# Attention layer on one core: the first two steps' probabilities are moved one step at a time, and three pair stores go to ScalarE's queue

## What is computed

```python
q = query @ w_q                       # 32 batches x 64 queries, 16 heads of 64
kv = context @ w_kv                   # 32 batches x 1601 keys, 192 channels in
scores = jnp.einsum('bhqd,bhkd->bhqk', q, k) * SCALE
attn = jax.nn.softmax(scores, axis=-1)
out = jnp.einsum('bhqk,bhkd->bhqd', attn, v)
```

## Time and profile before

| | |
|---|---|
| median of three runs | 2347.87 us (2347.65 to 2348.88) |
| the profiled execution | 2348.63 us, of which the span of instructions 2346.8 us |
| TensorE busy | 2290.6 us, 98% of the span |
| GpSimd, VectorE, ScalarE busy | 1647.7, 1815.5, 1541.4 us |
| DMA engines, SyncE's queue (q1) | 76.9% of 16 engines' span |
| start of the first scores / first product | 121.11 / 158.99 us |

### The profile page before, as it was taken

One profiled execution on the slowest core, in us unless ns is written; L12 is line 12 of the kernel. 1 busy time (PEld: TensorE's weight loads), 2 busy tenths in 40 slices (PEclk: granted clock), 3 DMA queues, 4 the chain that ended last, 5 costly groups with the idle time before them and its releaser, 6 DMA issues.

```text
span 2346.8 us, 43941 instructions
## 1 busy us (share of the span) xinstructions
PE 2290.6 (98%) x13696; PEld 2098.0 (89%) x13696; DVE 1815.5 (77%) x3664; ACT 1541.4 (66%) x2696; POOL 1647.7 (70%) x858
## 2 busy tenths in 40 slices
PE   7989999999999999999999999999999999899999
PEld 5769999999999999999999999999999998878788
DVE  7867777777777777777777777777777777789884
ACT  6756666666666666666666666666666666565444
POOL 4248888888888888888888888888888886421111
PEclk9999999999999999999999999999999999999999
DMA  8988888888888888888888888888888886987000
GB/s 228 261 222 197 195 191 199 199 199 199 199 198 199 200 199 200 199 200 199 200 199 201 199 200 199 199 200 200 200 200 199 200 197 157 212 202 197 1 10 28
DMA packets 410274, 438.97 MB, mean 187 GB/s; under 512 B 82529, under 2 KB 380897, under 8 KB 410209
## 3 DMA queue, kind: packets, MB, share of 16 engines
q1 hardware_dynamic: 391248, 425.66, 76.9%
q10 hardware_dynamic: 18960, 12.49, 2.3%
HBM read 167.42 MB, written 52.43 MB: 94 GB/s over the span
## 4 chain that ended last, share of the span: by engine, by line
PE 41%; POOL 31%; issue 17%; DVE 4%; SPq 3%; DMA 1%; ACT 1%; ACTq 0%; POOLq 0%; DVEq 0%
POOL p_pt_lo L667 17%; PE p_scores L1557 14%; PE p_acc L1577 9%; POOL p_nat L694 5%; PE p_acc L1579 4%; POOL p_q_lo L679 4%; POOL p_ct_lo L675 3%; POOL p_ct_hi L686 3%; SPq L462 2%; PE p_cols L1625 2%; PE p_scores L1683 2%; PE p_scores L1729 2%; PE p_cols L1716 2%; PE p_scores L1641 1%; PE p_scores L1507 1%
## 5 line engine op out<-in xcount | busy, mean ns | idle before, releaser
L667 POOL TENSOR_TENSOR p_pt_lo<-p_landed,p_pt_hi 128x768 fp32r<-128x768 f32 x504 | 991.0, 1987 | 326.3 <-ACT p_pt_hi L893 326.3
L1577 PE MATMUL p_acc<-p_nat,p_pt_hi 128*128 128x384 f32 x3024 | 890.4, 361 | 16.0 <-POOL p_pt_lo L667 14.8
L1579 PE MATMUL p_acc<-p_nat,p_pt_lo 128*128 128x192 f32 x3024 | 759.6, 251 | 0.0
L929 ACT ACTIVATE p_prob<-p_scores,p_negmax 128x800 f32<-128x800 f32 (+1 forms) x512 | 470.9, 925 | 382.5 <-DVE p_negmax L1266 382.5
L1557 PE MATMUL p_scores<-p_ct_hi,p_q_hi 128*128 128x512 f32 (+2 forms) x2048 | 703.0, 347 | 4.2 <-ACT p_prob L929 4.0
L1557 PE MATMUL p_scores<-p_ct_hi,p_q_lo 128*128 128x512 f32 (+2 forms) x2048 | 702.6, 346 | 0.0
L1577 PEld LDWEIGHTS p_acc<-p_nat,p_pt_hi 128*128 128x128 f32 x3024 | 569.3, 188 | 24.8 <-issue 14.1
L1579 PEld LDWEIGHTS p_acc<-p_nat,p_pt_lo 128*128 128x128 f32 x3024 | 578.8, 191 | 0.0
L893 ACT ACTIVATE p_pt_hi<-p_landed 128x768 fp32r<-128x768 f32 x504 | 398.6, 838 | 176.2 <-PE p_acc L1581 128.7
L1276 DVE STREAM_TRANSPOSE turned<-p_prob 128x1536 f32<-128x1536 f32 x256 | 452.6, 1768 | 0.0
L1557 PEld LDWEIGHTS p_scores<-p_ct_hi,p_q_hi 128*128 128x128 f32 x2048 | 388.4, 190 | 50.6 <-ACT p_prob L929 6.2
(11 more groups left out here) (253 smaller groups left out, 3128.6 us busy)
## 6 DMA issues: line engine op xcount, KB each, us to landing
p_landed<-turned SPq DMA_DIRECT2D x2032, 104.0 KB, 2.3
resid<-in_ctx SPq DMA_DIRECT2D x128, 288.0 KB, 5.0
o_scratch<-resid SPq DMA_DIRECT2D x256, 96.0 KB, 2.6
p_stage<-qk_scratch SPq DMA_DIRECT2D x31, 512.0 KB, 3.9
p_stage<-qk_scratch SPq DMA_DIRECT2D x62, 256.0 KB, 4.2
qk_scratch<-p_out_a SPq DMA_DIRECT2D x30, 512.0 KB, 5.3
p_stage<-in_ctxT SPq DMA_DIRECT2D x31, 401.0 KB, 4.7
p_stage<-in_ctxT SPq DMA_DIRECT2D x62, 200.5 KB, 5.6
```

What stands on the lines that cost most here:

```text
L667: nc.gpsimd.tensor_tensor(pt_lo[:, t0:t1, :, :], by_tile(slot, t0, t1), bits(pt_hi[:, t0:t1, :, :]), ALU.subtract).then_inc(pt_lo_done, 1)
L929: nc.scalar.activation(prob[:, lo:hi], scores[:, S0 + lo:S0 + hi], ACT.Exp, bias=negmax[:, par:par + 1], accum_out=rowsum[:, par, h:h + 1] ...
L1577: nc.tensor.matmul(acc[k % 2][:, 0:2 * DC], pt_hi[:, t, :, :].rearrange("p i x -> p (i x)"), x[:, t, :], start=t == 0, stop=False, skip_gr ...
L1579: nc.tensor.matmul(acc[k % 2][:, 0:DC], pt_lo[:, t, :, :].rearrange("p i x -> p (i x)"), x[:, t, 0:DC], start=False, stop=False, skip_grou ...
```

## The change

Three things. The first pair (steps 0 and 1) is moved by `move_first`, one step at a time: 16 DMAs for step 0 as soon as it is transposed, and 16 for step 1, with the two parts of `load_qk` around them. Staging slot 0 is laid one `landed` slot further back, so that `landed`'s first slot is free of it (slot 3, which is laid behind it, shifts as well). And pair 29 is stored by ScalarE too, in step 1. The waits follow: high(0) waits for `moved_first`, high(1) and all later for `moved` as before, and VectorE's step 4 waits for both.

```diff
+        assert put.at <= landed_at + 4 * PADDED
+        put.at = landed_at + 4 * PADDED
+        first_slot = slot(0)
         assert put.at >= landed_at + 2 * 4 * PADDED
         last_slot = slot(3)
...
+        def move_first(eng, j, done):
+
+            slot = slice(j, j + 1)
+            for i in range(G):
+                for g in range(G):
+                    dst = landed[g * R:(g + 1) * R, slot, i, :, :].rearrange("p s t x -> p s (t x)")
+                    eng.dma_start(dst, turned[i * R:(i + 1) * R, slot, g * GK:(g + 1) * GK]).then_inc(done, 16)
...
-                    if begins:
-                        sp.wait_ge(qk_stored[0], GP // SLOTS * 32)
-                    move(n * PPB, 0, begins)
+                    if not begins:
+                        move(n * PPB, 0, False)
...
-            for h in range(2):
-
-                sp.wait_ge(ct_a_done, 3 + h)
-                load_qk(1, h, stage[:, h, :])
-                store_queries(GP - LATE + 1 + h)
+
+            sp.wait_ge(ct_a_done, 3)
+            load_qk(1, 0, stage[:, 0, :])
+            store_queries(GP - LATE + 1)
+            sp.wait_ge(turned_done, 1)
+            move_first(sp, 0, moved_first)
+            sp.wait_ge(ct_a_done, 4)
+            load_qk(1, 1, stage[:, 1, :])
+            sp.wait_ge(turned_done, 2)
+            sp.wait_ge(qk_stored[0], GP // SLOTS * 32)
+            move_first(sp, 1, moved[0])
             passes(sp, body)
...
-                act.wait_ge(moved[slot // 2], count)
+                if fresh:
+                    act.wait_ge(moved_first, MOVES)
+                else:
+                    act.wait_ge(moved[slot // 2], count)
...
-                    if first and j in (LATE - 3, LATE - 2):
+                    if first and LATE - 4 <= j < LATE - 1:
                         g = GP - LATE + 1 + j
...
                 dve.wait_ge(exp_done, s + 1)
+                if first and j == 4:
+                    dve.wait_ge(moved_first, MOVES)
```

More of the change, by code:

```diff
@@ L227, in whole_layer @@
         slot = lambda i: (put(f"out_a{i}", [P, CB, 2, NQ]), put(f"out_b{i}", [DCB, CB, 2, NQ]))
-        first_slot = slot(0)
         x_ident = put("x_ident", [P, P])
         x_stats, x_mv, x_std = put("x_stats", [P, TT, 6]), put("x_mv", [P, TT, 2]), put("x_std", [P, 4, TT])
+        assert put.at <= landed_at + 4 * PADDED
+        put.at = landed_at + 4 * PADDED
+        first_slot = slot(0)
         assert put.at >= landed_at + 2 * 4 * PADDED
@@ L336, in whole_layer @@
         turned_done = sem("turned_done")
-        moved, moved_last = [sem("moved0"), sem("moved1")], [sem("moved_last0"), sem("moved_last1")]
+        moved_first, moved, moved_last = sem("moved_first"), [sem("moved0"), sem("moved1")], [sem("moved_last0"), sem("moved_last1")]
         pt_hi_done, pt_lo_done, last_lo_done = sem("pt_hi_done"), sem("pt_lo_done"), sem("last_lo_done")
```

## The result

Median of five runs: 2406.73 us (2405.74 to 2409.66) after, 2347.87 us (2347.17 to 2353.6) before, measured beside it. The ratio is 1.0252, with a 95% interval of 1.0241 to 1.0263: 58.9 us slower. I had forecast 2347.5 with a range to 2352.2.

The account below looks back on a forecast made before the run. TensorE's pace was taken as the bound, so only start-up idleness counted: 1.9 us gained at product(2) less 1.6 for the clock, 0.3 off the median 2347.87, giving 2347.5 us; own range 2344.8 to 2350, 8-in-10 range 2343.7 to 2352.2.

Parts of the forecast that it names:

- From there on all waits for TensorE's pace again: After product(2), later moves land ahead of need (182.0 against 184.2 us), so batches keep 58.46 us.
- the whole sum: At product(2): 1.9 us gained, 1.6 lost to the clock, leaving 0.3 us; no change forecast.
- Both signs that I had named for an error: Wrong if product(2) starts before 171 or after 177 us, or if later batches are not at 58.46 us.
- my rivals: Start-up alternatives: whole pause goes, 2340.5 us (with a milder way 0.12); full stalls, 2352.2 (0.17); every single stalls, 2358.4 (0.11).
- T: Time at which SyncE has issued the second single-step group of moves: forecast 153.3 us, 153.20 before.
- the rival in which the 5.7 us of stalls come back in full: SyncE's first moves: T 157.9, product(2) at 177.9, 4.3 us lost with the clock, 2352.2 us; chance 0.17.
- the rival after: Each single DMA stalls as the first move's did: T 164.1, product(2) at 184.1, 2358.4 us; chance 0.11.
- the issue of a single: SyncE's issue of single-step moves at the start: 10.6 us for each group of 16.
- the row of rows 7: Earlier trace's row for single-step DMAs, taken as the measure of the new groups: 16 issues in 10.58 us, median 592 ns.
- The 0.95 us for 64 KB: Skill figure cited against the change at the first moves: 15.2 us a group, T 162.5, some 9 us slower.
- 1.6 us lost in product(2): TensorE's clock falls in the 5.5 us pause before product(2), costing the same 1.6 us as before, now behind it.
- high(2) released by the landing: At the start, ScalarE's high(2) waits for the move of steps 2 and 3 to land, at about 170.4 us.

Follow-up runs that it names:

- split-only one: The kernel before with the first group's split and the slots' shift, third pair still stored by SyncE, loop start 334: 2353.38 us, ratio 1.002.
- 335: The whole changed kernel with 40 more do-nothing instructions ahead of SyncE's loop: 2350.21 us, ratio 1.0012 to the kernel before.
- 295: SyncE instructions ahead of its loop in the changed kernel, 2406.73 us, and in the kernel before with 13 more waits, 2402.91 us, ratio 1.023.
- 312: The kernel before with 30 more do-nothing instructions ahead of SyncE's loop: 2385.97 us, ratio 1.0155.
- 279: The kernel before with the slot shift and third pair stored by ScalarE, no split, no padding: 2347.30 us, ratio 0.9989.
- 282: SyncE instructions ahead of its loop in the kernel before, unedited: 2347.87 us.
- 287: The whole change without padding, half of the first step's 16 moves issued by ScalarE instead of SyncE: 2348.35 us, ratio 1.0004.
- 288: The kernel before with 6 more do-nothing instructions ahead of SyncE's loop: 2348.68 us, ratio 1.0001.
- 336: Three kernels with the second batch's six row loads issued by ScalarE: changed kernel 2347.85 us, kernel before 2346.42, store and slots without split 2345.09.
- 339: The kernel before with only the slots' shift and third pair stored by ScalarE, no split, padded: 2345.20 us, ratio 0.9982.
- 342: The kernel before with 60 more do-nothing instructions ahead of SyncE's loop: 2346.37 us, ratio 0.9989.

## Why the prediction was wrong

- **The step that failed** is "From there on all waits for TensorE's pace again", and with it the whole sum, which ended at product(2). I had treated the batches behind the start as untouched, since no instruction in them changed. Their place in SyncE's instruction memory changed, and each turn lost 4.15 us, 13 times. Both signs that I had named for an error came: batches not at their 58.46 us, which is this one, and product(2) after 177, which is the start's.
- **None of my rivals held it.** All of them worked on the start. I had counted the issues that the change adds in time, never in length of the code ahead of the loop, and I had not asked how much SyncE could lose in a turn. The trace of before had the answer to the second: 3.4 us in 117.
- **The start went by a rival, not by my forecast.** T was to be 153.3 and was 158.4; the rival in which the 5.7 us of stalls come back in full had 157.9. Product(2) was to be at 173.3 and came at 178.15, where that rival had 177.9. (T lies just past 158.3, from which on I had given it to the rival after, whose own T was 164.1.) The term that was mis-sized is the issue of a single: 13.86 and 11.82 us a group in place of 10.6 each, 4.5 us of the 5.1; the two issues of `load_qk` between them took 2.2 in place of 1.2. The group of the earlier trace rows had loads beside it on ScalarE's queue and no pair store; these had pair stores. That is 0.87 and 0.74 us an issue for 0.66 (where the prediction says that it takes the row of rows 7, rows 8 is meant).
  The 0.95 us for 64 KB that the Trainium skill lists (DMA: Bandwidth & Descriptors, section Bandwidth) is the time in which the DMA engines are busy with one transfer that GpSimd issued, so it was no measure of an issue. What an issue took here is 0.66 us in the group of the earlier trace rows, 0.74 and 0.87 in the changed kernel and 1.00 in the split-only one.
- **The clock was counted once and fell twice.** I had product(0) at full speed behind its shorter wait and 1.6 us lost in product(2). After a wait of only 2.24 us product(0) took 5.40 us too. It cost nothing at the end, since product(2) waited 5.2 us for the DMA anyway; in product(2) the loss was 1.8.
- **Right** were product(0) (153.0 for 153.2, its wait 2.24 for 2.2), high(2) released by the landing with a pause of 5.2 us behind it (5.5 forecast), and the clock at half in it (0.50 from 176 to 180 us).
- **With the loop's place taken out** the change costs 1.4 us (2350.21), within my range, but not by my sum. In the traces that kernel comes to its first branch 6.3 us later than the kernel before (372.9 for 366.7 us), gets 2.5 back in the 13 turns, which goes with its start of 335, and 3.8 behind the loop. The part behind the loop takes 454 to 461 us over the fourteen traces, and what sets it I have not found. So a start that lost more than the rival's 4.3 us still ended at 1.4 in the medians, and that this fell within my range is luck.

## What to carry over

A change ahead of a hardware loop moves the loop's code, and on an engine with a long loop body that alone can cost more than anything else the change does. Read the packets of the instruction queue and the gap behind the branch in a turn first; a few do-nothing instructions ahead of the loop tell place from content in one run. And ask of each engine how much it can lose in a turn, the ones that only issue included: SyncE's 3.4 us, and not TensorE's share, decided here.

## What the runs showed of the hardware

- A stall of 3.8 to 5.0 us at SyncE's branch and five packets of instructions in each turn, with 295 or 312 instructions ahead of a body of 293 records; none with 279, 282, 287, 288, 334, 335, 336, 339 or 342. The Trainium skill (Runtime: NRT & Kernel Launch, section Instruction fetch mechanics) has it that a taken branch out of the blocks held forces a fetch. The trace agrees, with 4.57 us behind the branch at 492.6.
- A pause of about 0.36 us of SyncE at every 128th instruction when it is reached for the first time, and in every turn of the loops that stall, there with one packet of 8 KB; in a loop that fetches nothing, 0.12 us.
- The same 16 issues of the first pair take two times. The kernel before took 16.02 us. Here are the one with the store and slots edit and, with nothing but waits added, the kernel before with 60 more:

```profile
136.96 16.03 SPq L473 DMA_DIRECT2D p_landed<-turned  x16
```

```profile
136.69 13.59 SPq L462 DMA_DIRECT2D p_landed<-turned  x16
```

  I saw 15.0 to 16.1 us in six profiled executions and 13.6 in three. High(0) then starts at 155.4 to 156.1 or at 152.4 to 152.7. The time turns up elsewhere: in the three, the second DMA of ScalarE's pair store at 142 to 143 us takes 2.2 to 2.5 us to issue, in the six 0.8 to 0.9. It looks as if one queue or the other is held while a pair store is under way; what decides which I have not found. Part of the kernel before's spread, 2342.8 to 2353.6 us over its runs, may be this; that is argued, not shown.
- Half the bytes do not halve an issue: whole single-step groups took 11.5 to 15.9 us while pair stores were under way and 10.58 at the end of the steps, and a group of two steps' slots 13.6 to 16.1 us there and 10.3 us once they were over.
